# Mixture-of-experts stages: chosen experts only, on rows scattered by place, instead of every expert on every row

## The chip, the cores and the metric

The kernel runs on one core of one Trainium2 chip. The metric is the time of one execution on the device, in microseconds (us). Engines are named as in the profile: PE is TensorE's matmul and PEld its weight load, DVE is VectorE, ACT is ScalarE, POOL is GpSimd, SP is SyncE (here it only starts DMAs).

## The reference

Two transformer layers over 2048 tokens of width 128, all float32. Each layer is an attention and a feed-forward part; layer 0 has a 16-head attention and a routed feed-forward, layer 1 an 8-head attention, a second 16-head attention and a routed feed-forward. The change touches the two routed feed-forwards:

```python
# layer 0: 8 experts, each token takes 2; expert width 384; and one shared expert of width 128
top_v, top_i = jax.lax.top_k(probs, 2)
gates = jax.nn.softmax(top_v, axis=-1)
for e in range(8):
    out = out + comb[:, e, None] * swiglu(normed, gate_up_w[e], down_w[e])   # comb: gate or 0
out = out + swiglu(normed, shared_gate_up_w, shared_down_w)
# layer 1: 4 experts, each token takes 1; expert width 512
expert_idx = jnp.argmax(logits, axis=-1)
for e in range(4):
    gate_raw, value = jnp.split(h @ expert_wv[e], 2, axis=-1)
    y = silu(gate_raw) * value @ expert_proj[e]
    out = out + jnp.where((expert_idx == e)[..., None], y, 0.0)
```

`swiglu(h, wg, wd)` is `(silu(gate) * up) @ wd.T` with `gate, up` the halves of `h @ wg.T`.

## The kernel before

The 2048 tokens are 16 tiles (`NT`) of 128 rows, or 4 blocks (`NB`) of 512 (`BLK`). The program is a chain of stages; in each, every engine runs its own list, tied by semaphores, and a barrier stands between two stages. No scheduler orders anything around the change: each engine does what its list says, in that order. Around a routed feed-forward the stages are `project_norm_route` (output projection, layer norm, transposed and scaled copy `hT` of the normed rows, router logits, and `routing` on DVE, which leaves in `comb` one weight per token and expert, zero for experts not chosen), then `experts`, then a norm (`norm_l2_norm` in layer 0, `final_norm` in layer 1).

`experts` runs twice: tag `e0` with E = 8 experts of NF = 3 chunks of 128 (and the shared expert as a ninth), tag `e1` with E = 4 and NF = 4. It computes every expert on every token. A unit is one expert on one block of 512 tokens. In `up` (L886 to L893) PE multiplies, for each of the NF chunks, the gate and the up weights with 512 columns of `hT` (L891, L892). ACT takes the silu of the gate half (L932), DVE multiplies it with the up half (L950). In `dn` (L895 to L901) PE multiplies 128-column pieces of that product with the down weights (L900), 4·NF matmuls of 128 columns, and DVE's `gather` (L955 to L962) adds the result, times `comb`, to the running sum (L960). PE's list has `up` of a unit ahead of `dn` of the unit before it. Loops over pairs of experts are hardware loops (`Fori`). The weights lie in two slots; SP loads the pair for the next turn (L848 and L849, two DMAs per expert) when the last unit of a slot is done, three quarters of a turn before it is wanted. The first two experts' weights are loaded during the stage that prepares the attention.

Of the kernel before, what the change touches and what calls it, by code (L numbers as in the profile page):

```python
# [16 lines left out]
BF16 = mybir.dt.bfloat16  # L17
ALU = mybir.AluOpType
# [3 lines left out]
P = 128  # L22
# [4 lines left out]
TPB = BLK // P  # L27
HEADS, HD = 16, 8
# [65 lines left out]
def small_head_operands(core, tag, src_T, w, bias, cs, arrived, KS, QS, V, place, kbias, tokens, opening, later):  # L94
# [7 lines left out]
    with ExitStack() as st:  # L102
# [23 lines left out]
        with nc.Block() as block:  # L126
# [9 lines left out]
            @block.gpsimd  # L136
            def _(pool):
                if opening:
                    opening.gpsimd(pool)
                pool.memset(V[:, :, :, HD:], 1.0).then_inc(ones_set, 1)  # L140
                for s in range(NS):
# [499 lines left out]
def routing(dve, act_pair, chain, lg, prob, cand, pick, comb, rank, small, n_exp, top2):  # L641
# [19 lines left out]
    if not top2:  # L661
        first_of(lg, m, comb)
        return
# [20 lines left out]
    step(dve.tensor_tensor(pick[:, 0], pick[:, 0], wide(g1), ALU.mult))  # L684
    step(dve.tensor_tensor(pick[:, 1], pick[:, 1], wide(g2), ALU.mult))
    step(dve.tensor_tensor(comb, pick[:, 0], pick[:, 1], ALU.add))
# [19 lines left out]
def project_norm_route(core, tag, OT, X, XA, hT, comb, w, w_in, E, post_norm, top2):  # L706
# [9 lines left out]
    with ExitStack() as st:  # L716
        sem = lambda n: core.sem(st, f"{tag}_{n}")
        sb = lambda n, s, dt=F32: core.sb(st, f"{tag}_{n}", s, dt)
        N = sb("N", [P, NT, P])
# [4 lines left out]
        pick = sb("pick", [P, 2, NT, E])  # L724
        small = sb("small", [P, 5, NT])
# [7 lines left out]
        with nc.Block() as block:  # L733
# [54 lines left out]
            def _(dve):  # L788
# [39 lines left out]
                routing(dve, (e_in, e_out), chain, lg[:, :, :], prob, cand, pick, comb[:, :, 0:E], w["rank"], small, 0, top2)  # L828
                if top2:
                    chain.link(dve.memset(comb[:, :, E:E + 1], 1.0))  # L830
                chain.settle()


class ExpertTiles:
# [3 lines left out]
    def __init__(self, core, st, tag, gate_up, down, NF, shared):  # L838
        self.gate_up, self.down, self.shared, F = gate_up, down, shared, NF * P
        sb = lambda n, s: core.sb(st, f"{tag}_{n}", s)  # L840
        self.wgu, self.wd = sb("wgu", [P, 2, 2 * F]), sb("wd", [P, 2, NF, P])
        self.sgu, self.sd = (sb("sgu", [P, 2 * P]), sb("sd", [P, P])) if shared else (None, None)
        self.w_in = [core.sem(st, f"{tag}_w_in{s}") for s in range(2)]
        self.s_in = core.sem(st, f"{tag}_s_in")

    def load(self, sp, slot, e):
        one = slice(e, e + 1) if isinstance(e, int) else bass.ds(e, 1)
        sp.dma_start(self.wgu[:, slot, :], self.gate_up[one].rearrange("o d f -> (o d) f")).then_inc(self.w_in[slot], 16)  # L848
        sp.dma_start(self.wd[:, slot, :, :], self.down[one].rearrange("o (c p) n -> p (o c) n", p=P)).then_inc(self.w_in[slot], 16)  # L849

    def load_first(self, sp):
        self.load(sp, 0, 0)
        self.load(sp, 1, 1)
        if self.shared:
            sp.dma_start(self.sgu[:, :], self.shared[0]).then_inc(self.s_in, 16)
            sp.dma_start(self.sd[:, :], self.shared[1]).then_inc(self.s_in, 16)


def experts(core, tag, hT, comb, acc, tiles, E, NF):
# [4 lines left out]
    shared, wgu, wd, sgu, sd, w_in, s_in = (tiles.shared, tiles.wgu, tiles.wd, tiles.sgu, tiles.sd, tiles.w_in, tiles.s_in)  # L864
    with ExitStack() as st:
        sem = lambda n: core.sem(st, f"{tag}_{n}")
        sb = lambda n, s, dt=F32: core.sb(st, f"{tag}_{n}", s, dt)
        gate = sb("gate", [P, 2, BLK])
        prod = sb("prod", [P, 2, NF, BLK])

        gu_ready, gu_free, silu_done, prod_ready = (sem(n) for n in ("gu_ready", "gu_free", "silu_done", "prod_ready"))
        y_ready, y_free = sem("y_ready"), sem("y_free")
        UNITS = 2 * NB
        PAIRS = E // 2

        with nc.Block() as block:
            @block.sync
            def _(sp):
                with sp.Fori(0, PAIRS - 1) as it:
                    for slot in range(2):  # L880
                        sp.wait_ge(y_ready, it * UNITS + NB * (slot + 1))
                        tiles.load(sp, slot, it * 2 + 2 + slot)

            @block.tensor
            def _(pe):
                def up(wts, nf, n, u, b):  # L886
                    for c in range(nf):
                        pe.wait_ge(gu_free, n + c + 1)
                        bank = 2 * ((u * nf + c) % 2)
                        cols = hT[:, b * BLK:(b + 1) * BLK]  # L890
                        pe.matmul(ps[:, bank, :], wts[:, c * P:(c + 1) * P], cols, start=True, stop=True)  # L891
                        pe.matmul(ps[:, bank + 1, :], wts[:, (nf + c) * P:(nf + c + 1) * P], cols,  # L892
                                  start=True, stop=True).then_inc(gu_ready, 1)  # L893

                def dn(wts, nf, n, u, m):  # L895
                    pe.wait_ge(prod_ready, n + nf)
                    pe.wait_ge(y_free, m + 1)
                    for i in range(TPB):
                        for c in range(nf):
                            mm = pe.matmul(ps[:, 4 + u % 2, i * P:(i + 1) * P], prod[:, u % 2, c, i * P:(i + 1) * P],  # L900
                                           wts(c), start=(c == 0), stop=(c == nf - 1))  # L901
                    mm.then_inc(y_ready, 1)

                with pe.Fori(0, PAIRS) as it:
                    n0, m0 = it * (UNITS * NF), it * UNITS
                    for u in range(UNITS):
                        slot = u // NB
                        if u % NB == 0:
                            pe.wait_ge(w_in[slot], it * 32 + 32)
                        up(wgu[:, slot, :], NF, n0 + u * NF, u, u % NB)  # L910
                        if u >= 1:
                            v = u - 1
                            dn(lambda c: wd[:, v // NB, c, :], NF, n0 + v * NF, v, m0 + v)
                    v = UNITS - 1
                    dn(lambda c: wd[:, v // NB, c, :], NF, n0 + v * NF, v, m0 + v)
                if shared:
                    n0, m0 = PAIRS * UNITS * NF, PAIRS * UNITS
                    pe.wait_ge(s_in, 32)
                    for u in range(NB):
                        up(sgu[:, :], 1, n0 + u, u, u)  # L920
                        if u >= 1:
                            dn(lambda c: sd[:, :], 1, n0 + u - 1, u - 1, m0 + u - 1)
                    dn(lambda c: sd[:, :], 1, n0 + NB - 1, NB - 1, m0 + NB - 1)

            @block.scalar
            def _(act):
                def silu(nf, n, u):
                    for c in range(nf):
                        k = (u * nf + c) % 2
                        act.wait_ge(gu_ready, n + c + 1)  # L930
# [863 lines left out]
```

## Time and profile before

| | us |
|---|---|
| three runs, median | 2432.5 |
| three runs, lowest and highest | 2427.86 and 2433.84 |
| the profiled execution | 2438.78 |
| its span, first to last instruction | 2436.9 |
| first expert stage (layer 0, tag e0) | 265.8, from 793.5 to 1059.3 |
| second expert stage (layer 1, tag e1) | 171.9, from 2249.5 to 2421.4 |
| routing on DVE ahead of the first expert stage | from 784.7 to 792.9 |

The profile gives the instructions of one execution with their start and duration, the time an engine sat idle before an instruction and what ended that idle time. A float32 matmul stands in it as two records. The granted clock (PEclk) is the share of TensorE's full 2.4 GHz that was granted; 0.5 is the 1.2 GHz level.

### The profile page before, as it was taken

The page shows a single profiled execution, that of the slowest core. Times are in us where ns is not written, and L with a number is a line of the kernel's source. Part 1 is how long each engine was busy: PE and PEld are TensorE (multiplying, and loading weights), DVE is VectorE, ACT ScalarE, POOL GpSimd, SP SyncE. Part 2 cuts the span into 40 slices and gives each one's busy share as a digit, 9 for nine tenths or more (in the row PEclk, how much of TensorE's full clock was granted, in tenths as well). Part 3 has the DMA queues.
Part 4 walks back from the last instruction along what each step waited for, and adds up shares of the span by engine and source line. Part 5 has one row for each costly group of instructions (what it writes and reads, how often), then busy time and mean ns, then how long its engine had stood idle before and what let it go on. Part 6 is the DMA issues. An engine that isn't in the chain of part 4 may idle for free. (4 is left out here: it accounts for less than half of the span.)

```text
span 2436.9 us, 41652 instructions
## 1 busy us (share of the span) xinstructions
PE 2136.9 (88%) x16528; PEld 1019.0 (42%) x16528; DVE 1684.9 (69%) x2408; ACT 1398.9 (57%) x2564; POOL 208.1 (9%) x366
## 2 busy tenths in 40 slices
PE   7589999999995999968897999996759999996997
PEld 2122222222223566644565776775212323343564
DVE  4799999999944344444765677775479888862334
ACT  3179989899894222234544566563417888773221
POOL 2000000000001000012331111111100000000000
PEclk7589999999997999989998999998659999996998
DMA  3000000000000000000000000001000000000000
GB/s 109 1 3 4 6 4 6 4 6 6 4 6 3 10 20 19 10 35 1 1 1 1 1 1 1 1 1 42 26 1 4 4 6 6 9 10 10 14 13 17
DMA packets 21424, 26.01 MB, mean 11 GB/s; under 512 B 4736, under 2 KB 14976, under 8 KB 21120
## 3 DMA queue, kind: packets, MB, share of 16 engines
q1 hardware_dynamic: 19152, 21.42, 3.1%
q8 instruction: 120, 1.97, 0.3%
q10 hardware_dynamic: 2096, 2.17, 0.3%
q14 instruction: 56, 0.46, 0.1%
HBM read 17.94 MB, written 1.05 MB: 8 GB/s over the span
## 5 line engine op out<-in xcount | busy, mean ns | idle before, releaser
L591 ACT ACTIVATE a0a_probs<-psum 128x512 f32<-128x512 f32 x1024 | 554.0, 596 | 109.2 <-PE psum L531 102.2
L615 DVE TENSOR_REDUCE a0a_mx<-psum 128x2 f32<-128x1024 f32 x512 | 583.2, 1213 | 9.2 <-PE psum L511 8.9
L511 PE MATMUL psum<-a_KS,a_QS 48*128 48x512 bf16 (+3 forms) x1664 | 332.9, 393 | 78.6 <-DVE a0a_mx L615 42.7
L591 ACT ACTIVATE a1a_probs<-psum 128x512 f32<-128x512 f32 (+3 forms) x640 | 304.6, 533 | 118.5 <-PE psum L531 77.7
L615 DVE TENSOR_REDUCE a1a_mx<-psum 128x2 f32<-128x1024 f32 (+2 forms) x320 | 323.8, 1060 | 53.1 <-PE psum L511 30.0
L531 PE MATMUL psum<-a_QS,a_KS 51*128 51x512 bf16 (+3 forms) x1664 | 337.4, 382 | 10.9 <-ACT a1a_probs L591 4.1
L554 PE MATMUL psum<-a0a_probs,a_V 128*16 128x256 f32 x4096 | 327.1, 391 | 7.8 <-ACT a0a_OD L580 5.5
L932 ACT ACTIVATE e_gate<-psum 128x512 f32<-128x512 f32 x164 | 97.9, 597 | 320.7 <-PE psum L892 320.7
L1284 PE MATMUL psum<-b_VW,b_ST 128*128 128x129 f32 x2176 | 256.2, 280 | 16.2 <-DVE X L1395 16.2
L1284 PEld LDWEIGHTS psum<-b_VW,b_ST 128*128 128x128 f32 x2176 | 253.1, 197 | 17.3 <-DVE X L1395 17.3
L1264 PE MATMUL psum<-b_GT,AT 128*128 128x512 f32 (+3 forms) x640 | 244.8, 536 | 16.9 <-ACT b_ST L1323 16.9
L531 PEld LDWEIGHTS psum<-a_QS,a_KS 51*128 51x128 bf16 x1664 | 87.2, 93 | 368.6 <-ACT a0a_probs L591 197.0
L950 DVE TENSOR_TENSOR e_prod<-e_gate,psum 128x512 f32<-128x512 f32 x164 | 112.8, 688 | 181.5 <-ACT e_gate L932 181.5
L1371 DVE TENSOR_TENSOR b_M<-b_M,b_ST 128x512 f32<-128x512 f32 (+3 forms) x288 | 176.0, 611 | 51.6 <-ACT b_ST L1323 19.2
L1264 PEld LDWEIGHTS psum<-b_GT,AT 128*128 128x128 f32 x640 | 122.4, 193 | 154.3 <-issue 115.5
L554 PE MATMUL psum<-a1a_probs,a_V 128*16 128x256 f32 (+1 forms) x2304 | 179.3, 382 | 4.2 <-ACT a1a_OD L580 4.1
L1330 ACT ACTIVATE b_ST<-b_ST 128x2048 f32<-128x2048 f32 x48 | 91.8, 1912 | 153.9 <-DVE b_ST L1379 153.9
L1323 ACT ACTIVATE b_ST<-psum 128x512 f32<-128x512 f32 (+1 forms) x320 | 156.2, 536 | 36.3 <-PE psum L1264 35.1
L900 PEld LDWEIGHTS psum<-e_wd,e_prod 128*128 128x128 f32 x1280 | 149.6, 192 | 20.0 <-issue 20.0
L900 PE MATMUL psum<-e_wd,e_prod 128*128 128x128 f32 x1280 | 149.7, 275 | 0.0
L554 PEld LDWEIGHTS psum<-a0a_probs,a_V 128*16 128x16 f32 x4096 | 68.6, 95 | 193.3 <-issue 99.2
L511 PEld LDWEIGHTS psum<-a_KS,a_QS 48*128 48x128 bf16 x1664 | 83.4, 95 | 149.9 <-DVE a0a_mx L615 76.0
(202 smaller groups left out, 1929.7 us busy)
## 6 DMA issues: line engine op xcount, KB each, us to landing
e_wgu<-in_l_gate_up SPq DMA_DIRECT2D x8, 384.0 KB, 3.0
a_cs<-in_rope ACTq DMA_DIRECT2D x4, 512.0 KB, 9.9
a_cs<-in_rope SPq DMA_DIRECT2D x1, 2048.0 KB, 7.5
e_wgu<-in_l_gate_up SPq DMA_DIRECT2D x4, 512.0 KB, 3.5
e_wd<-in_l_down SPq DMA_DIRECT2D x8, 192.0 KB, 3.0
AT<-in_xT SPq DMA_DIRECT2D x4, 256.0 KB, 6.1
a_QS<-a0a_mrow SPq DMA_DIRECT2D x64, 3.0 KB
a0a_num<-a0a_OD SPq DMA_DIRECT2D x64, 16.0 KB
```

What stands on the lines that cost most here:

```text
L511: mm = pe.matmul(ps[:, 2 * slot + half, 0:width], QS[rows, 2 * p + i, q_cols(qb, qt * P, P)], KS[rows, 2 * p + i, c * BLK:c * BLK + width] ...
L531: mm = pe.matmul(ps[:, S_BANK + e % S_SLOTS, c:BLK], KS[rows, 2 * p + i, kt * P:(kt + 1) * P], QS[rows, 2 * p + i, q_cols(qb, c, BLK - c)] ...
L554: mm = pe.matmul(ps[32 * j:32 * j + 2 * HD, AV_BANK, a:b], V[:, kt, HPP * p + j, :], probs[:, e % P_SLOTS, a:b], start=(kt == 0 and half = ...
L591: act.activation(probs[:, e % P_SLOTS, c:BLK], ps[:, S_BANK + e % S_SLOTS, c:BLK], ACT.Exp, scale=scale).then_inc(exp_done, 1)
L615: dve.tensor_reduce(mx[:, pk % 2, qt, 2 * i:2 * i + 2, c], banks, AX.X, ALU.max).then_inc(max_done, 1)
L900: mm = pe.matmul(ps[:, 4 + u % 2, i * P:(i + 1) * P], prod[:, u % 2, c, i * P:(i + 1) * P], wts(c), start=(c == 0), stop=(c == nf - 1))
L932: act.activation(gate[:, k, :], ps[:, 2 * k, :], ACT.Silu).then_inc(silu_done, 1)
L950: dve.tensor_tensor(prod[:, u % 2, c, :], gate[:, k, :], ps[:, 2 * k + 1, :], ALU.mult).then_inc(prod_ready, 1)
L1264: pe.matmul(ps[:, n % S_BANKS, c:BLK], xnT[:, kt * P:(kt + 1) * P], GT[:, a % 3, c:BLK], start=True, stop=True).then_inc(s_ready, 1)
L1284: mm = pe.matmul(ps[:, O_BANK + i // 2, cols], ST[:, plan.at[a][kt // TPB], kt % TPB, i * P:(i + 1) * P], VW[:, kt, h, :], start=(kt == 0 ...
L1323: act.activation(tile(a, kt), ps[:, n % S_BANKS, c:BLK], ACT.Copy).then_inc(copied, 1)
L1371: dve.tensor_tensor(M[:, a % 2, c:], M[:, a % 2, c:], tile(a, kt), ALU.max).then_inc(max_done, 1)
```

## The change

`ExpertTiles` and `experts` go; `sparse_experts`, with `SharedExpert`, `Route`, `Dispatch` and the constant `dispatch_table`, takes their place. The tokens are cut in two halves (`PARTS`). Within a half, each token is given a row number for each expert it chose (K = 2 in layer 0, 1 in layer 1), such that the rows of one expert stand together and each expert begins at a multiple of 128. That takes at most JT = 8·K + E − 1 tiles of 128 rows: 23 in layer 0 and 11 in layer 1, of which some are empty; all are computed, 46 and 22 in all.

- DVE and PE work out the row numbers (`posi`) and which expert each tile belongs to (`own`): four matmuls and some 14 small DVE operations.
- POOL scatters the normed rows N of each token tile, once per choice, to `xg` in device memory with an indirect DMA (32 in layer 0, 16 in layer 1), and at the end gathers the results from `yg` back, by as many indirect DMAs.
- SP reads the tile's expert number from SBUF into a register, waits until the slot is free (three slots, freed by `y_ready` of the tile three before), and fetches all of that expert's weights with one DMA (now merged in one array, 576 KB in layer 0, 768 KB in layer 1), once for each tile. SP also loads the scattered rows and stores the results in groups of four tiles.
- PE transposes the tile's 128 rows (`turn`), ACT scales them, then `up`, silu, product and `down` run on 128 columns; DVE copies the result to `yout` (`keep`). The choice's weight is applied after the gather (`collect`), in layer 0 by one DVE operation per token tile and choice, in layer 1 by a plain add.
- The shared expert runs ahead of the tiles. `xg` is filled with zeros at the start of the kernel. The last three operations of `routing` and a memset go.

```diff
+                def load_weights(j):
+                    e = sp.value_load(own[0:1, j // JT, j % JT:j % JT + 1], min_val=0, max_val=E - 1)
+                    if j >= SLOTS:
+                        sp.wait_ge(y_ready, S + j - SLOTS + 1)
+                    sp.dma_start(W[:, j % SLOTS, :], weights[bass.ds(e, 1)].rearrange("o p n -> (o p) n")).then_inc(w_in[j % SLOTS], 16)
+                def load_rows(b):
+                    sp.wait_ge(sent[b], 16 * K * PART_TILES)
+                    for c, (lo, hi) in enumerate(CHUNKS):
+                        rows = xg[b][lo * P:hi * P, :].rearrange("(t p) c -> p t c", p=P)
+                        sp.dma_start(xin[:, b, lo:hi, :], rows).then_inc(x_in[b][c], 16)
+                def store(b, g):
+                    lo, hi = GROUPS[g]
+                    sp.wait_ge(y_free, S + JT * b + hi)
+                    rows = yg[b][lo * P:hi * P, :].rearrange("(t p) c -> p t c", p=P)
+                    sp.dma_start(rows, yout[:, b, lo:hi, :]).then_inc(stored[b], 16)
...
+                for b in range(PARTS):
+                    for t in tiles_of(b):
+                        for k in range(K):
+                            pool.indirect_dma_start(xg[b], bass.IndirectOffsetOnAxis(posi[:, k, t:t + 1], 0),
+                                                    route.N[:, t, :], None).then_inc(sent[b], 16)
+                for b in range(PARTS):
+                    pool.wait_ge(stored[b], 16 * len(GROUPS))
+                    for t in tiles_of(b):
+                        for k in range(K):
+                            pool.indirect_dma_start(G[:, k, t, :], None, yg[b],
+                                                    bass.IndirectOffsetOnAxis(posi[:, k, t:t + 1], 0)).then_inc(back[t // TPB], 16)
...
+                def turn(j):
+                    b, i = divmod(j, JT)
+                    for c, (lo, hi) in enumerate(CHUNKS):
+                        if i == lo:
+                            pe.wait_ge(x_in[b][c], 16)
+                    if j >= 2:
+                        pe.wait_ge(x_ready, j - 1)
+                    pe.transpose(ps[:, 6 + j % 2, 0:P], xin[:, b, i, :], core.ident[:, :]).then_inc(turned, 1)
+                def up(j):
+                    n, s = S + j, j % SLOTS
+                    wait_banks(n)
+                    pe.wait_ge(w_in[s], 16 * (j // SLOTS + 1))
+                    pe.wait_ge(x_ready, j + 1)
+                    for half in range(2):
+                        for c in range(NF):
+                            mm = pe.matmul(ps[:, 2 * half + n % 2, c * P:(c + 1) * P],
+                                           W[:, s, half * F + c * P:half * F + (c + 1) * P], xT[:, j % 2, :], start=True, stop=True)
+                    mm.then_inc(gu_ready, 1)
+                def down(j):
+                    n, s = S + j, j % SLOTS
+                    wait_down(n)
+                    for c in range(NF):
+                        mm = pe.matmul(ps[:, 4 + n % 2, 0:P], prod[:, n % 2, c * P:(c + 1) * P],
+                                       W[:, s, 2 * F + c * P:2 * F + (c + 1) * P], start=(c == 0), stop=(c == NF - 1))
+                    mm.then_inc(y_ready, 1)
...
+                turn(0)
+                for j in range(ALL):
+                    if j + 1 < ALL:
+                        turn(j + 1)
+                    up(j)
+                    if j:
+                        down(j - 1)
+                down(ALL - 1)
...
+                        for t in range(g * TPB, (g + 1) * TPB):
+                            ins = dve.scalar_tensor_tensor(out=acc[:, t, :], in0=G[:, k, t, :], scalar=route.small[:, 3 + k, t:t + 1],
+                                                           in1=acc[:, t, :], op0=ALU.mult, op1=ALU.add)
```

The list of SP in the first expert stage, before: the two DMAs of an expert's weights (`e_wgu` gate and up, `e_wd` down) behind one wait for PE.

```order
L848 ISA [waits e0_y_ready]
L848 DMA e_wgu<-in_l_gate_up 128x768
L849 ISA
L849 DMA e_wd<-in_l_down 128x3x128
```

The same list now, at the fifth to seventh tile: `e0_own` is the expert number, `e0_W` the slot, `e0_yout` a group of results.

```order
L943 TENSOR_LOAD e0_own
L943 ISA x2
L946 ISA [waits e0_y_ready]
L946 DMA e0_W<-in_l0_experts 128x1152
L958 DMA yg0<-e0_yout 128x4x128 [waits e0_y_free]
L943 TENSOR_LOAD e0_own
L943 ISA x2
L946 ISA [waits e0_y_ready]
L946 DMA e0_W<-in_l0_experts 128x1152
```

Where SP issued 6 such pairs in the stage (and 2 in advance), it now issues 46 loads, each behind a wait for the `down` three tiles back; the register read stands ahead of the wait.

PE's list in the first expert stage, before (`e_wgu`, `e_wd` weights, `h0T` the transposed rows): the last chunk of one unit's `up`, then the 12 matmuls of `dn`.

```order
L891 MATMUL psum<-h0T,e_wgu 128x512 [waits e0_gu_free]
L892 MATMUL psum<-h0T,e_wgu 128x512
L897 ISA [waits e0_prod_ready]
L900 MATMUL psum<-e_wd,e_prod 128x128 [waits e0_y_free]
L900 MATMUL psum<-e_wd,e_prod 128x128 x11
```

The same list now, one tile and the beginning of the next: `e_xin` are the gathered rows, `e_xT` their transpose.

```order
L1031 MATMUL psum<-ident,e_xin 128x128 [waits e0_x_ready]
L1040 MATMUL psum<-e_xT,e_W 128x128 [waits e0_x_ready,e0_w_in1,e0_prod_ready]
L1040 MATMUL psum<-e_xT,e_W 128x128 x5
L1048 MATMUL psum<-e_W,e_prod 128x128 [waits e0_y_free,e0_prod_ready]
L1048 MATMUL psum<-e_W,e_prod 128x128 x2
L1031 MATMUL psum<-ident,e_xin 128x128 [waits e0_x_ready]
```

Every tile now waits for its own weights (`e0_w_in`), once for 10 matmuls of 128 columns; before, one such wait stood ahead of 4 units of 18 matmuls each.

POOL had nothing in the stage. Its list there now (`d_N` normed rows, `e_posi` row numbers, `e_G` the gathered results):

```order
L981 DMA xg<-d_N,e_posi 2944x128 [waits blank,e0_pos_ready]
L981 DMA xg<-d_N,e_posi 2944x128 x31
L987 DMA e_G<-yg,e_posi 128x128 [waits e0_stored0]
L987 DMA e_G<-yg,e_posi 128x128 x15
L987 DMA e_G<-yg,e_posi 128x128 [waits e0_stored1]
L987 DMA e_G<-yg,e_posi 128x128 x15
```

The first 16 scatters stand ahead of the first tile, and the last 16 gathers behind the last one.

## Rows read from the trace of the kernel before

**Rows 1.** The page: busy time, share of the span and instruction count of each engine.
```profile
PE 2136.9 (88%) x16528; PEld 1019.0 (42%) x16528; DVE 1684.9 (69%) x2408; ACT 1398.9 (57%) x2564; POOL 208.1 (9%) x366
```

**Rows 2.** Busy time by stretch (start:end length, engines, PEclk, DMA share, GB/s): both expert stages.
```profile
793.50:1059.30 265.80, 263.79 (x1200) 162.90 (x1200) 109.29 (x244) 64.84 (x104) 0.00 (x0) 0.99 0.04 14
2249.50:2421.40 171.90, 170.15 (x768) 104.03 (x768) 62.06 (x128) 40.74 (x66) 0.02 (x1) 0.98 0.03 9
```

**Rows 3.** Grouped instructions, first expert stage: count | busy, mean ns | idle before <-releaser.
```profile
L891 PE MATMUL psum<-h0T,e_wgu 128*128 128x512 f32 x192 | 99.8, 601 | 9.1 <-DVEq L942 9.1
...
L900 PE MATMUL psum<-e_wd,e_prod 128*128 128x128 f32 x768 | 90.3, 275 | 0.0
...
L932 ACT ACTIVATE e_gate<-psum 128x512 f32<-128x512 f32 x100 | 59.7, 597 | 197.7 <-PE psum L892 197.7
```

**Rows 4.** In order of time (start, duration): a unit boundary in the first expert stage.
```profile
854.81 3.74 PE L900 MATMUL psum<-e_wd,e_prod 128*128 128x128 f32 x32
...
858.75 0.34 SPq L848 DMA_DIRECT2D e_wgu<-in_l_gate_up  x1
...
859.27 0.38 SPq L849 DMA_DIRECT2D e_wd<-in_l_down  x1
...
868.72 2.84 PE L900 MATMUL psum<-e_wd,e_prod 128*128 128x128 f32 x24
```

**Rows 5.** DMA issues: KB each, median us from issue to landing.
```profile
e_wgu<-in_l_gate_up SPq DMA_DIRECT2D x8, 384.0 KB, 3.0
...
e_wgu<-in_l_gate_up SPq DMA_DIRECT2D x4, 512.0 KB, 3.5
...
e_wd<-in_l_down SPq DMA_DIRECT2D x4, 256.0 KB, 3.9
...
out_tokens<-XA SPq DMA_DIRECT2D x4, 256.0 KB, 2.2
big_raw<-in_l_big_wq SPq DMA_DIRECT2D x1, 512.0 KB, 3.5
...
big_raw<-in_l_big_wo SPq DMA_DIRECT2D x1, 512.0 KB, 6.1
a_wk<-in_l_wk SPq DMA_DIRECT2D x2, 64.0 KB, 1.8
```

**Rows 6.** SP's queue in order of time, first and last of four 512 KB loads.
```profile
1059.54 0.34 SPq L1005 DMA_DIRECT2D big_raw<-in_l_big_wq  x1
...
1060.88 0.43 SPq L1005 DMA_DIRECT2D big_raw<-in_l_big_wo  x1
```

**Rows 7.** POOL's groups over the whole span, columns as in rows 3.
```profile
L1215 POOL PARTITION_ALL_REDUCE b_row<-b_M x32 | 57.0, 1783 | 33.1 <-DVE b_M L1371 27.4 <-issue 5.7
...
L740 POOL TENSOR_TENSOR r_scales<-r_both,r_half 128x4 f32<-128x4 f32 x4 | 4.1, 1030 | 9.7 <-DVE r_both L802 9.7
```

**Rows 8.** DVE in order of time, end of the first routing.
```profile
792.14 0.29 DVE L685 TENSOR_TENSOR r_pick<-r_pick,r_small 128x128 f32<-128x128 f32 x1
792.47 0.29 DVE L686 TENSOR_TENSOR comb<-r_pick 128x128 f32<-128x128 f32 x1
```

**Rows 9.** Four PE transposes of 128x128, in order of time.
```profile
768.85 0.66 PE L756 MATMUL psum<-ident,r_N 128*128 128x128 f32 x4 [3.49 <-DVE r_N L816]
```

**Rows 10.** Groups over the whole span, 128x384 and 128x128 forms on ACT and DVE.
```profile
L1371 DVE TENSOR_TENSOR b_M<-b_M,b_ST 128x384 f32<-128x384 f32 x32 | 19.1, 596 | 8.5 <-POOL b_ST L1207 7.0
...
L591 ACT ACTIVATE a1a_probs<-psum 128x128 f32<-128x128 f32 x64 | 14.2, 275 | 9.4 <-PE psum L487 9.4
```

**Rows 11.** Busy time by stretch, columns as in rows 2: stretches that bear on TensorE's clock.
```profile
302.00:305.40 3.40, 1.71 (x22) 0.42 (x14) 3.40 (x2) 2.81 (x6) 0.00 (x0) 1.00 0.00 0
306.00:312.00 6.00, 4.50 (x30) 0.72 (x34) 4.93 (x5) 1.47 (x3) 0.00 (x0) 0.50 0.00 0
1139.00:1142.50 3.50, 1.97 (x5) 0.66 (x5) 1.88 (x5) 2.03 (x5) 0.00 (x0) 1.00 0.00 0
795.00:797.00 2.00, 2.00 (x4) 0.82 (x3) 0.00 (x0) 0.00 (x0) 0.00 (x0) 0.50 0.00 0
```

More of the change, by code:

```diff
@@ L827, in _ @@
                 chain.settle()
[L828 to L843, printed above, removed]
-        self.s_in = core.sem(st, f"{tag}_s_in")
[L846 to L856, printed above, removed]
@@ new lines, in _ @@
+                sp.wait_ge(own_ready, 1)
+                for j in range(SLOTS):
+                    load_weights(j)
+                load_rows(0)
+                stores = [(JT * b + GROUPS[g][1], b, g) for b in range(PARTS) for g in range(len(GROUPS))]
+                for j in range(SLOTS, ALL):
+                    if j % JT == JT - GROUP and j // JT + 1 < PARTS:
+                        load_rows(j // JT + 1)
+                    load_weights(j)
+                    while stores and stores[0][0] + SLOTS <= j:
+                        store(*stores.pop(0)[1:])
@@ new lines, in _ @@
+                for _, b, g in stores:
+                    store(b, g)
+            @block.gpsimd
+            def _(pool):
+                pool.wait_ge(pos_ready, 1)
+                pool.wait_ge(*blank)
+                for b in range(PARTS):
[9 more added lines that the diff above has]
+                                                    bass.IndirectOffsetOnAxis(posi[:, k, t:t + 1], 0)).then_inc(back[t // TPB], 16)
@@ L933, in _, with silu @@
[L933 to L938 removed]
+                def silu(n, width):
+                    act.wait_ge(gu_ready, n + 1)
+                    if n >= 2:
+                        act.wait_ge(prod_ready, n - 1)
+                    act.activation(gate[:, n % 2, 0:width], ps[:, n % 2, 0:width], ACT.Silu).then_inc(silu_done, 1)
@@ L955, in gather @@
-                def gather(m, u, b, e):
-                    dve.wait_ge(y_ready, m + 1)
-                    one = slice(e, e + 1) if isinstance(e, int) else bass.ds(e, 1)
-                    for i in range(TPB):
-                        t = b * TPB + i
-                        ins = dve.scalar_tensor_tensor(out=acc[:, t, :], in0=ps[:, 4 + u % 2, i * P:(i + 1) * P],
-                                                       scalar=comb[:, t, one], in1=acc[:, t, :],
-                                                       op0=ALU.mult, op1=ALU.add)
-                    ins.then_inc(y_free, 1)
@@ L964, in _ @@
[L964 to L976 removed]
+                chain = Chain(dve, sem("chain"))
@@ new lines, in _ @@
+                for u in range(S):
+                    product(u, BLK)
+                    if u:
+                        add_shared(u - 1)
+                if S:
+                    add_shared(S - 1)
+                at = {JT + JT // 2 + 1: 0, JT + 3 * JT // 4 + 1: 1} if PARTS == 2 else {}
+                for j in range(ALL):
+                    product(S + j, F)
+                    if j:
+                        keep(j - 1)
+                    if j in at:
+                        collect(at[j])
@@ L1646, in two_layers @@
         forward = list(range(NB))
+        rows = (PART_TILES * 2 + 7) * P
+        xg, yg = ([nc.dram_tensor(f"{n}{b}", (rows, P), F32, kind="Internal").ap() for b in range(PARTS)] for n in ("xg", "yg"))
         with ExitStack() as layer:
```

326 lines of the change are left out of this document (220 added, 106 removed).

## Prediction

> **What bounds the kernel now.** I looked first at the engines' busy shares, then at the stages the change touches. PE is busy 88% of the span [rows 1], but only the two expert stages matter here. There the view by stretch shows PE busy 263.8 of 265.8 us and 170.2 of 171.9 us, while DVE and ACT are busy under half of the time and the DMA engines 4% [rows 2]. The reader is to see that both stages are bound by PE at the full clock (0.99 and 0.98), and that weight traffic is nothing: each expert's weights serve 2048 rows. The groups of the first stage say what fills PE: matmuls of 512 columns (the one line shown, and its twin for the up half), and 768 records (384 matmuls) of 128 columns [rows 3]. So fewer rows through PE do shorten these stages, until something else is late. Of 8 (4) experts, 2 (1) are needed per token; with padding the change computes 46 tiles of 128 rows where 128 stood, and 22 where 64 stood.
>
> **Price of a tile on PE.** In order of time, 24 records (12 matmuls of 128 columns) take 2.84 us and 32 take 3.74 us, 0.234 us a matmul with its weight load hidden [rows 4]. Four transposes take 0.66 us with the tail of the last, which I read as 0.12 us each [rows 9]. A tile of layer 0 is one transpose, 6 `up` and 3 `down`: 0.12 + 9·0.234 = 2.23 us. In layer 1 it is 0.12 + 12·0.234 = 2.93 us. ACT's silu and scaling (two operations between 0.28 and 0.60 us) and DVE's product and copy (0.60 us for 128x384, some 0.3 us for 128x128) come to under 1.1 us a tile [rows 3, 10] and hide behind that. Were PE the bound, the loops would take 46·2.23 = 103 and 22·2.93 = 64 us.
>
> **Price of a tile by its weights.** Every tile now fetches its own weights, and load j may start only when `down` of tile j−3 is done. Four 512 KB loads were issued between 1059.54 and 1060.88 [rows 6]; the first landed 3.5 us and the last 6.1 us after its issue [rows 5], that is at 1063.0 and 1067.0: three further loads in 3.95 us, 1.3 us for 512 KB. So a load costs 2.2 us fixed and 1.3 us per 512 KB: 3.67 us for 576 KB and 4.15 us for 768 KB. (As two DMAs 0.52 us apart the 768 KB took 0.52 + 3.9 = 4.4 us [rows 4, 5]; that is my upper end.) To it come 0.16 us from the last matmul's issue to its end (275 ns of one record against 117 ns spacing [rows 3, 4]), 0.2 us from that end to SP's issue (858.55 to 858.75 [rows 4]), and an estimated 0.1 us to wake PE: 4.13 and 4.61 us. In PE's list there lie between `down` of tile j−3 and `up` of tile j one whole period and one transpose. The period is so 4.13 − 0.12 = **4.0 us** in layer 0 and **4.5 us** in layer 1, against 2.23 and 2.93 us of PE work. The weights, not PE, end each wait. SP's register read is new and in no row; it stands ahead of the wait and has some 3 us to hide in.
>
> The Trainium skill, "DMA: Bandwidth & Descriptors", section "Anatomy of one DMA — SWDGE (gpsimd) path", fits a DMA to 2.0 us plus its bytes at 436 GB/s; as an estimate that is 3.35 and 3.8 us a load, and by it the two loops would be some 23 us shorter. The row with 512 KB (3.5 us where the fit says 3.2) is longer than that.
>
> **Loops.** 46·4.0 = 184 and 22·4.5 = 99 us. Stores of 256 KB (0.65 us of the DMA engines each at the rate above) and the loads of further rows share the DMA engines with the weights, 12 and 6 stores: I add 6 and 3 us. Loops: 190 and 102 us.
>
> **What stands ahead of the first tile.** (a) Row numbers: 9 small DVE steps of about 0.32 us spacing (0.33 us from 792.14 to 792.47 for the like [rows 8]), some wider, and two trips to PE: 5.0 us, in layer 1 4.5. (b) 16 scatters on POOL in layer 0, 8 in layer 1; the shared expert (10 us on PE) runs beside them and is hidden, and so are the first three weight loads. The trace shows no indirect DMA. Ends: SP's issue of a DMA, 0.33 us [rows 4], and the longest software operation of POOL, 1.78 us; a tiny POOL power takes 1.03 us [rows 7]. It cannot be below nothing, since POOL does nothing here now. I take **1.3 us**, between the two POOL rows because POOL builds each of the 128 row transfers itself: 20.8 and 10.4 us. (c) The last scatter lands (2.2 us, as a store to device memory), the first three tiles of rows are loaded (between 1.8 us for 64 KB and 3.0 for 384 KB [rows 5], 2.4), transposed and scaled (0.8): 5.4 us.
>
> **What stands behind the last tile.** `down` and copy 1.1 us (1.3), store 2.2, gathers of the second half on POOL 20.8 (10.4), landing 2.2, the last sums 2.8 (0.7): 29.1 and 16.8 us. The gathers of the first half run beside the second half's tiles and cost nothing while the loop is this slow.
>
> **The sum.** Layer 0: 5.0 + 20.8 + 5.4 + 190 + 29.1 = 250.3 against 265.8, −15.5. Layer 1: 4.5 + 10.4 + 5.4 + 102 + 16.8 = 139.1 against 171.9, −32.8. `routing` loses three steps, −1.0 [rows 8]. Zero-filling `xg` (3 MB) happens in the opening, where nothing of the next 700 us waits for it: 0. Together −49.3 us: the profiled execution's 2438.8 becomes 2389.5. It stands 6.3 us above the median of the three runs, so I forecast **2384**.
>
> **What each unknown is worth.** 48 indirect DMAs lie on the path: 1 us more on each is 48 us. The loops have 68 tiles: 0.1 us more on each is 7 us. POOL's ends give −47 and +23; the loads' ends (3.5 us as for 512 KB, 0.25 us more as for two DMAs) −12 and +17.
>
> **Rivals.**
> 1. *POOL is cheap.* 0.6 us an indirect DMA: 48·0.7 = 34 us less, **2350**. For it: SP issues in 0.33 us. Against: POOL's own rows. The Trainium skill, "SBUF — State Buffer", section "A bandwidth-pool intuition that's wrong (but worth ruling out)", states 620 ns for a DMA of this kind alone, and 3100 ns beside a DVE copy that holds the port which POOL needs; by the first the time would be 2351, by the second 2470. No row here shows either.
> 2. *POOL is dear: slower than before.* If a scatter or gather of 128 rows costs over 2.3 us, the 48 on the path eat the whole gain; at 2.6 us the time is **2446**. For it: an all-reduce takes 1.78 us and a power on 4 columns 1.03 us [rows 7], so 128 separately addressed rows may well cost more; and DVE works beside it, on the shared expert's products. Against: nothing but those same rows' size.
> 3. *The clock falls.* With the tail of its matmuls counted as the profile counts it, PE would be about 2.5 of 4.0 us busy in layer 0's loop. A stretch with about 55% busy (1139 to 1142.5) keeps the full clock; one with 50% busy (302 to 305.4) is followed by one at half (306 to 312), which ends while PE is full; and the first 2 us after the idle time ahead of the first expert stage run at half (795 to 797) [rows 11]. [...] At 1.2 GHz a tile's PE work is at most doubled, 4.5 and 5.9 us, so at most 0.5·46 + 1.4·22 = 54 us more; but then PE is full, which is what brings the clock back. I take half: **2410**.
> 4. *The loads hide.* Had weight loads no effect, the loops would run at PE's pace, 81 + 35 = 116 us less: **2268**. Against: no row of such a size lands under 3.5 us, and only three slots are there.
> 5. *SP is late.* If the register read and its checks took over 3.3 us, SP would set the period; at 4.5 us in layer 0 that is 23 us more, and with 1 us for each store and row load, which stand in the same list, some 13 more: **2420**.
>
> **How the numbers follow.** Chances: forecast 0.47 (its own range 2355 to 2412), cheap POOL 0.19, dear POOL 0.13, clock 0.11, loads hidden 0.03, SP late 0.07. Range **2325 to 2440**: it takes in POOL's lower end together with 12 us from the loads, and reaches beyond the clock and SP cases; loads hidden and most of dear POOL are left out. A measurement of this kernel tells 0.3% (7.3 us) from no change. Faster by more: 0.82. Within: 0.05. Slower by more: 0.13.
>
> **What would show it.** Right: the DMA queue moving some 45 MB of weights; in both loops PE busy 55 to 65%, its idle time ended by the weights' DMA, and tiles 4.0 and 4.5 us apart; `y_ready` to SP's issue 0.2 us and issue to landing 3.6 and 4.2 us; two stretches of some 20 us in the first stage and two of 10 us in the second in which only POOL works. Wrong: idle time of PE ended by ACT or DVE (then the chain within a tile is the bound), POOL's spacing outside 1.0 to 1.8 us, or SP's issue long after `y_ready`.

## The result and the profile after

The changed kernel took **2336.6 us** (median of 4 runs, 2334.42 to 2344.91) against 2432.4 (4 runs, 2427.86 to 2433.84): ratio 0.9616, 95% interval 0.9589 to 0.9642. The forecast was 2384; the gain is 96 us where 48 were forecast. The profiled execution took 2337.2 us, its span is 2335.4.

From the page of the changed kernel, the engines' shares and the DMA issues (KB each, median us to landing):

```profile
PE 1899.2 (81%) x16048; PEld 934.0 (40%) x16048; DVE 1591.9 (68%) x2242; ACT 1364.8 (58%) x2536; POOL 300.5 (13%) x463
...
e_W<-in_l_experts SPq DMA_DIRECT2D x46, 576.0 KB, 4.0
e_W<-in_l_experts SPq DMA_DIRECT2D x22, 768.0 KB, 4.4
```

PE lost 238 us of busy time [rows 1], and 44 MB of weights are loaded in the two stages. The two expert stages cut into what stands ahead of the first tile, the loop, and what stands behind it (windows of the changed kernel; span of each, busy time of the engines, granted clock, DMA share, GB/s):

```profile
789.84:820.93 31.09, 15.77 (x58) 9.48 (x59) 9.99 (x23) 4.23 (x7) 19.54 (x20) 0.72 0.35 114
820.93:980.24 159.31, 114.18 (x870) 105.89 (x871) 39.20 (x107) 42.76 (x91) 26.73 (x29) 0.95 0.67 206
980.24:1008.49 28.25, 0.44 (x4) 0.25 (x3) 4.88 (x17) 0.00 (x0) 15.10 (x16) 0.56 0.17 44
2193.46:2214.44 20.98, 2.92 (x10) 2.04 (x11) 3.02 (x15) 0.60 (x2) 12.50 (x13) 0.50 0.51 173
2214.44:2304.24 89.80, 70.45 (x548) 67.34 (x548) 20.71 (x45) 23.66 (x44) 10.67 (x12) 0.93 0.62 201
2304.24:2319.73 15.49, 0.00 (x0) 0.00 (x0) 1.72 (x3) 0.00 (x0) 7.56 (x9) 0.63 0.17 47
```

Beside the forecast's terms:

| us | forecast | measured |
|---|---|---|
| layer 0, ahead of the first tile | 31.2 | 31.1 |
| layer 0, 46 tiles | 190 | 159.3 |
| layer 0, behind the last tile | 29.1 | 28.3 |
| layer 1, ahead | 20.3 | 21.0 |
| layer 1, 22 tiles | 102 | 89.8 |
| layer 1, behind | 16.8 | 15.5 |
| both stages | 389.4 | 344.9 |

The four outer terms are right within 2 us. The two loops hold 43 of the 44.5 us by which the stages beat the forecast. Outside the stages the span is 8.7 us shorter: `routing` 2.3, the first stage of the kernel 2.7, and 4.8 in layer 1's projections and small-head attention, of which 1.1 go back elsewhere. The last two are no work of the change. In the thirteen changed and experimental kernels profiled here, whose code there is the same, that stretch of layer 1 takes either some 510 us (seven of them, 509.2 to 510.8) or some 515 (six, 514.9 to 515.5; before 514.95), and the first norm stage starts anywhere from 754.2 to 760.9 (before 760.0). Each kernel has one profile, so whether this falls by chance or goes with the kernel is not shown.

Why a tile takes less than forecast can be read off three tiles. PE's list in layer 0's loop, changed kernel (start, duration, line; in brackets the idle time before it and what ended it). Each tile is a transpose (L1031), `up` (L1040), and the `down` (L1048) of the tile before:

```profile
899.52 1.58 PE L1040 MATMUL psum<-e_xT,e_W 128*128 128x128 f32 x12 [1.79 <-issue]
900.94 0.83 PE L1048 MATMUL psum<-e_W,e_prod 128*128 128x128 f32 x6
901.61 0.27 PE L1031 MATMUL psum<-ident,e_xin 128*128 128x128 f32 x1
902.50 1.58 PE L1040 MATMUL psum<-e_xT,e_W 128*128 128x128 f32 x12 [0.63 <-DVE e_prod L1135]
903.92 0.83 PE L1048 MATMUL psum<-e_W,e_prod 128*128 128x128 f32 x6
904.59 0.27 PE L1031 MATMUL psum<-ident,e_xin 128*128 128x128 f32 x1
905.99 1.58 PE L1040 MATMUL psum<-e_xT,e_W 128*128 128x128 f32 x12 [1.12 <-DVE e_prod L1135]
```

and SP's list beside it:

```profile
901.95 0.34 SPq L946 DMA_DIRECT2D e_W<-in_l_experts  x1
...
904.93 0.34 SPq L946 DMA_DIRECT2D e_W<-in_l_experts  x1
```

The `down` that ends at 901.77 frees a slot; 0.18 us later SP issues the load; the `up` that needs it starts at 905.99, 4.04 us after the issue. But that `down` stands right behind the `up` of 899.52, and from there to 905.99 are **two** tiles: 6.47 = 2.25 (`up` and `down`) + 0.18 + 4.04. The tile between them, at 902.50, waited 0.63 us for a load of its own, which had been under way since 897.80 and landed at 902.41. The profile puts that wait down to `e_prod`, which was done before 900.94; the weights had come last. It is so nearly everywhere: of the 29 tiles from the fourth on in layer 0 for which the trace has the landing, 27 begin `up` 0.09 us after it. Two loads are in flight beside each other, and half of the 6.47 us is a tile's share. In general, with s slots, s − 1 distances = `up` + `down` (2.25 in layer 0, 2.92 in layer 1) + 0.18 to the issue + landing + 0.09, or 2.5 us + landing in layer 0.

### The profile page after: what moved, and what is told of

Read it like the earlier page. It is cut to its first block and busy times, and to the rows that moved or that the text cites. A ratio compares the mean times of both kernels' runs of the same rounds, so it can differ in the third digit from the quotient of the medians.

```text
span 2335.4 us, 40174 instructions
## 1 busy us (share of the span) xinstructions
PE 1899.2 (81%) x16048; PEld 934.0 (40%) x16048; DVE 1591.9 (68%) x2242; ACT 1364.8 (58%) x2536; POOL 300.5 (13%) x463
## 5 line engine op out<-in xcount | busy, mean ns | idle before, releaser
L620 DVE TENSOR_REDUCE a1a_mx<-psum 128x2 f32<-128x1024 f32 (+2 forms) x320 | 323.7, 1060 | 51.9 <-PE psum L516 29.1
L1135 DVE TENSOR_TENSOR e_prod<-e_gate,psum 128x384 f32<-128x384 f32 (+1 forms) x72 | 43.4, 602 | 220.5 <-ACT e_gate L1074 220.5
L1040 PE MATMUL psum<-e_xT,e_W 128*128 128x128 f32 x904 | 126.3, 296 | 64.3 <-issue 39.8
L1040 PEld LDWEIGHTS psum<-e_xT,e_W 128*128 128x128 f32 x904 | 115.8, 206 | 75.9 <-issue 43.5
L1582 DVE TENSOR_TENSOR b_ST<-b_ST,b_row 128x2048 f32<-128x2048 f32 x48 | 107.8, 2288 | 40.8 <-POOL b_row L1418 40.8
```

Source lines behind the costliest of these rows:

```text
L620: dve.tensor_reduce(mx[:, pk % 2, qt, 2 * i:2 * i + 2, c], banks, AX.X, ALU.max).then_inc(max_done, 1)
L1040: mm = pe.matmul(ps[:, 2 * half + n % 2, c * P:(c + 1) * P], W[:, s, half * F + c * P:half * F + (c + 1) * P], xT[:, j % 2, :], start=True ...
L1582: dve.tensor_tensor(group, group, row[:, a % 2, :].unsqueeze(1).broadcast_to([P, TPB, BLK]), ALU.subtract).then_inc(wide_sub, 1)
```

## The experiments

Three theories of the distance between tiles. **One load at a time**, the prediction's: distance = landing + 0.1. **Two in turn**, the rule just read: 2·distance = 2.5 + landing. **Transfer rate**: 576 KB cannot come more often than every 3.4 us. All edits are to the changed kernel, and its 2336.6 us are what they are set beside.

### Four slots

```diff
-    SLOTS = 3
+    SLOTS = 4
```

> One change: the expert stages' weights have 4 slots in place of 3, so that the load of tile j is issued after the down of tile j-4. Three theories of what sets the tiles' distance (3.47 us in layer 0, 4.06 us in layer 1 in the changed kernel). One load at a time, as the prediction had it: distance = landing + 0.1 with three slots, half of that with four, so TensorE's own work sets it, 2.55 us and 3.2 us. Two in turn: the up of tile j waits for a load that was issued after the up and down that began with the up of tile j-2, so two distances = 2.5 + landing (4.0 to 4.6 us), with four slots three distances, 2.2 to 2.4 us, again under TensorE's work: 2.55 to 2.8 and 3.2 us. Both give 46 x 0.8 + 22 x 0.9 = 57 us less, 2280 us (2270 to 2295). Transfer rate (576 KB cannot land faster than every 3.4 us): no gain, 2337 us.

Measured: 2281.2 us (ratio to before 0.9379, 0.9364 to 0.9394). The loops take 122.1 and 67.9 us. Loads land later, 5.1 us in the median, and yet tiles come 2.26 us apart (median; mean 2.64). The transfer rate is no bound at 3.4 us: it falls. The other two forecast the same here, so this run does not choose between them.

### No loads in the loop

```diff
                 for j in range(SLOTS, ALL):
                     if j % JT == JT - GROUP and j // JT + 1 < PARTS:
                         load_rows(j // JT + 1)
-                    load_weights(j)
...
-                    pe.wait_ge(w_in[s], 16 * (j // SLOTS + 1))
+                    pe.wait_ge(w_in[s], 16)
```

> Leaves out the loads of weights from the fourth tile of each expert stage on, with their register reads: tiles use what the first three loads left in the slots. If the loads set the tiles' distance, what is left is TensorE's work of a tile with the turn of the next, 2.55 to 2.8 us in layer 0 and 3.2 us in layer 1: 2280 us (2270 to 2295). If the chain turn, scale, up, Silu, product, down sets it, the distance stays at 3.4 to 3.5 us and the time at 2337 us.

Measured: 2256.0 us (0.9273, 0.9259 to 0.9287). PE's list without loads:

```profile
849.92 1.50 PE L1039 MATMUL psum<-e_xT,e_W 128*128 128x128 f32 x12
851.26 0.83 PE L1047 MATMUL psum<-e_W,e_prod 128*128 128x128 f32 x6
851.93 0.27 PE L1030 MATMUL psum<-ident,e_xin 128*128 128x128 f32 x1
852.04 1.50 PE L1039 MATMUL psum<-e_xT,e_W 128*128 128x128 f32 x12
```

and the loop's window:

```profile
817.57:917.17 99.60, 99.09 (x872) 98.70 (x872) 38.75 (x107) 42.83 (x91) 26.78 (x29) 0.99 0.25 74
```

PE is full, 2.12 us a tile (2.79 in layer 1), under the 2.23 of the prediction and well under the 2.55 that I had written for this run, which is why the time is 14 us under the range expected. Nothing but the loads, with SP's register reads, stands between the changed kernel's 159.3 us and 99.6: the chain of ACT and DVE within a tile is hidden.

### Half of each load

```diff
-                    sp.dma_start(W[:, j % SLOTS, :], weights[bass.ds(e, 1)]...
+                    n = 3 * F if j < SLOTS else 3 * F // 2
+                    sp.dma_start(W[:, j % SLOTS, 0:n], weights[bass.ds(e, 1), :, 0:n]...
```

> From the fourth tile of each expert stage on only the first half of the weights' columns is loaded (288 and 384 KB); the rest of a slot keeps what the first loads brought. Landing should fall from 4.0 to about 3.25 us and from 4.4 to about 3.4 us. One load at a time (distance = landing + 0.1): 3.35 and 3.5 us, 2336.6 - 46 x 0.12 - 22 x 0.56 = 2319 us. Two in turn (distance = (2.5 + landing)/2, layer 1 (3.2 + landing)/2): 2.9 and 3.3 us, 2336.6 - 26 - 17 = 2294 us. Transfer rate: half the distance, so TensorE's own, 2280 us.

Measured: 2301.8 us (0.9449, 0.9431 to 0.9468). Window of layer 0's loop:

```profile
821.44:955.01 133.57, 108.42 (x872) 101.28 (x872) 39.02 (x107) 42.77 (x91) 26.77 (x29) 0.98 0.54 150
```

Landing fell to 3.1 us, tiles come 2.77 us apart in the median (mean 2.89); two in turn says (2.5 + 3.1)/2 = 2.8. The loop lost 25.7 us where 26 were expected by that theory and 5.5 by the other, and layer 1's lost 13.9 of 17. The total is 8 us over the 2294: 3 are those of layer 1, and the profiled execution has the 515 us form of the stretch named above; the rest is not accounted for. One load at a time falls: the distance, 2.77 us, is under the landing of 3.1, as it was under it in the changed kernel (3.35 and 4.0). A landing 0.86 us shorter took 0.57 us off a tile (by the medians), where the rule gives 0.43: it fits the level better than the slope.

### Two slots

```diff
-    SLOTS = 3
+    SLOTS = 2
```

> Two slots in place of three: the load of tile j is issued after the down of tile j-2, and the up of tile j follows it at once, so distance = TensorE's 2.3 (3.0) + 0.2 + landing: with 3.4 to 4.0 us of landing 5.9 to 6.5 us in layer 0, with 4.0 to 4.4 us 7.2 to 7.6 us in layer 1: 2336.6 + 46 x 2.7 + 22 x 3.3 = 2533 us (2515 to 2555). If the transfer rate sets the distance (3.4 us per 576 KB), one load at a time still lands in under 3.4 us and the loss is smaller than 100 us.

Measured: 2661.4 us (1.0937, 1.0917 to 1.0957, from two runs), over 100 us above every theory. PE's and SP's lists, and the loop's window:

```profile
905.75 2.90 PE L1040 MATMUL psum<-e_xT,e_W 128*128 128x128 f32 x12 [3.78 <-issue]
908.45 1.49 PE L1048 MATMUL psum<-e_W,e_prod 128*128 128x128 f32 x6
909.73 0.42 PE L1031 MATMUL psum<-ident,e_xin 128*128 128x128 f32 x1
913.80 2.90 PE L1040 MATMUL psum<-e_xT,e_W 128*128 128x128 f32 x12 [3.65 <-issue]
```

```profile
910.11 0.34 SPq L946 DMA_DIRECT2D e_W<-in_l_experts  x1
```

```profile
824.20:1188.22 364.02, 190.97 (x869) 177.38 (x870) 42.02 (x107) 42.82 (x91) 26.70 (x29) 0.64 0.30 92
```

`up` and `down` take 4.19 us where they took 2.25: PE runs at 1.2 GHz, and it is busy only 191 of 364 us even so. 4.19 + 0.17 + 3.69 = 8.05 us is the distance from 905.75 to 913.80; at the full clock it would be 6.1, within what was expected. The landing (3.7 us) is what was expected too. So the rule holds, and the miss is the clock, granted at 0.64 over this loop: the prediction's third rival, which did not come with three slots (0.95 granted, PE 72% busy), came in the run with the longer waits. No run keeps the longer waits and the lower clock apart; the 6.1 us are worked out, not measured.

### Every load twice

```diff
-        W = sb("W", [P, SLOTS, 3 * F])
+        W = sb("W", [P, SLOTS, 6 * F])
...
+                    sp.dma_start(W[:, j % SLOTS, 3 * F:6 * F], weights[bass.ds(e, 1)]...
```

> Every load of weights is done twice, the second time into a second half of a slot that nobody reads; a tile waits for both. Three slots. Landing of the later of the two perhaps 5.5 us (layer 0) and 6.4 us (layer 1). Two in turn: distances (2.5 + 5.5)/2 = 4.0 and (3.2 + 6.4)/2 = 4.8 us: 2336.6 + 46 x 0.5 + 22 x 0.75 = 2377 us; the check is the sum by the landing that the profile then shows. One load at a time: distance = landing + 0.1, 5.6 and 6.5 us: 2336.6 + 98 + 54 = 2490 us. Transfer rate (twice the distance): 2336.6 + 160 + 89 = 2585 us.

Measured: 2453.1 us (1.0084, 1.0055 to 1.0113, from two runs), under the 2490 and 2585 of the other two and 76 above the 2377. Tiles come 4.85 us apart in the median. From its first issue to the `up` a pair of loads took 6.2 us in the median, so 6.1 to landing, not 5.5; with that, two in turn gives 4.3 at the full clock and 5.3 at half, and the clock was 0.80 in this loop. The mean distance is 5.27, since two tiles at its start came 13.6 and 9.3 us after their neighbours and a later one 12.7, which no theory of the loads covers; more of that below. The run speaks against one load at a time (6.2) but is too disturbed to measure the slope.

### One part in place of two halves

```diff
-PARTS = 2
+PARTS = 1
```

> All the rows as one part in place of two halves: 39 and 19 tiles in place of 46 and 22, but all 32 and 16 scatters stand ahead of the first tile and all 32 and 16 gathers behind the last. At 1.26 us for each indirect transfer of 128 rows: 16 and 8 more on either side, 48 x 1.26 = +60 us; 7 x 3.45 and 3 x 4.06 us of tiles less, -36 us: 2336.6 + 24 = 2361 us (2350 to 2370). If GpSimd's transfers weren't what the stage's head and tail wait for: 2336.6 - 36 = 2300 us.

Measured: 2357.8 us (0.9688, 0.967 to 0.9706), 3 us from the expectation. Windows of layer 0, ahead, loop, behind:

```profile
792.23:843.44 51.21, 15.47 (x58) 9.48 (x59) 9.66 (x23) 4.24 (x7) 31.15 (x32) 0.63 0.26 89
843.44:975.59 132.15, 96.77 (x739) 89.36 (x739) 29.42 (x77) 36.18 (x77) 0.00 (x0) 0.95 0.64 194
975.59:1023.57 47.98, 0.00 (x0) 0.00 (x0) 9.46 (x33) 0.00 (x0) 30.32 (x32) 0.54 0.18 48
```

20.1 us more ahead and 19.7 behind for 16 indirect transfers each: 1.25 us a piece, all on the path. In layer 1 it is 9.1 and 10.1 for 8 each. The halves hide 48 transfers, worth 59 us, for ten padded tiles, 40 us.

### Plain transfers in place of indirect ones

```diff
-    pool.indirect_dma_start(xg[b], bass.IndirectOffsetOnAxis(posi[:, k, t:t + 1], 0), route.N[:, t, :], None)
+    pool.dma_start(xg[b][at:at + P, :], route.N[:, t, :])
...
-    pool.indirect_dma_start(G[:, k, t, :], None, yg[b], bass.IndirectOffsetOnAxis(posi[:, k, t:t + 1], 0))
+    pool.dma_start(G[:, k, t, :], yg[b][at:at + P, :])
```

> Scatters and gathers by GpSimd are plain transfers of the same 128 rows to and from fixed places, in place of indirect ones; the rows thus go to tiles by place and not by expert. 48 of the 96 stand on the path (16 + 16 + 8 + 8), 1.26 us each. If the price is that of reading 128 indices, a plain one should take GpSimd 0.6 us or less: at least 48 x 0.65 = 31 us less, 2305 us or under. If it is that of any transfer that GpSimd issues: 2337 us.

Measured: 2311.5 us (0.9497, 0.9479 to 0.9515). POOL's list of the changed kernel, then of this one:

```profile
808.70 0.96 POOL L981 DMA_INDIRECT xg<-d_N,e_posi  x1 [0.30 <-issue]
809.96 0.96 POOL L981 DMA_INDIRECT xg<-d_N,e_posi  x1 [0.30 <-issue]
```

```profile
797.91 17.16 POOL L982 DMA_DIRECT2D xg<-d_N  x32 [20.28 <-DVE e_posi L1121]
```

An indirect transfer of 128 rows holds POOL for 1.26 us, a plain one to or from 128 rows that stand together for 17.16/32 = 0.54. So 0.72 of the 1.26 us go with the indices and the scattered places, which this run changes together; the time is 6 us over the bound expected for that case and 26 under the other. Of 48·0.72 = 35 us, 24 came out at the stages' ends (7.9, 11.7, 1.1 and 3.7). Least came ahead of layer 1's first tile, where POOL was no longer last: it had issued the eighth scatter by 2187.1, but that landed at 2193.26, beside the first three loads of weights (2184.85 to 2196.0), and SP loads the rows behind it. Over both stages a plain scatter landed after 4.7 us where the indirect one took 2.6 (medians).

### More slots, and a stall

> Six slots for the weights. With four the loop's distances were 2.12 us where TensorE went at its own pace and 2.64 in the mean (layer 1 2.79 and 3.02). Loads that are issued five tiles ahead should be covered: 46 x 0.45 + 22 x 0.15 = 24 us less than with four slots, 2257 us, which is what the kernel without loads took (2256). If many loads in flight only slow each other and the rows' stores, the time stays at 2281 us.

Measured with `SLOTS = 6`: 2299.0 us (0.9455, 0.9433 to 0.9477), slower than with four. Most tiles do come 2.12 us apart, but three of them 10.9, 9.2 and 14.8 us after their neighbours. ACT's list there, and what its waits were put down to over the stage:

```profile
833.74 0.49 ACT L1074 ACTIVATE e_gate<-psum 128x384 f32<-128x384 f32 x1 [9.25 <-remote]
837.26 0.46 ACT L1080 ACTIVATE e_xT<-psum,columns 128x128 f32<-128x128 f32 x1 [3.03 <-PE psum L1031]
844.31 0.49 ACT L1074 ACTIVATE e_gate<-psum 128x384 f32<-128x384 f32 x1 [6.59 <-remote]
...
ACT e_gate L1074 <- remote: 30.5, 4, 12.2
```

and beside it one `down` on PE, POOL's last scatter and SP's next load:

```profile
834.88 1.65 PE L1048 MATMUL psum<-e_W,e_prod 128*128 128x128 f32 x6 [6.44 <-issue]
...
838.62 0.96 POOL L981 DMA_INDIRECT xg<-d_N,e_posi  x1 [0.31 <-issue]
...
844.53 3.09 SPq L946 DMA_DIRECT2D e_W<-in_l_experts  x2
```

The silu at 833.74 needed the `up` that had ended at 826.99; from 828.4 on, when PE has done one more `up`, POOL's list alone goes on. In the second stall SP stands as well: its load at 844.53 waited for the `down` that had ended at 836.53, where 0.18 us is usual. POOL's last scatter was over at 839.58, yet ACT and SP went on only at 844.3 and 844.5, so POOL's being busy is not by itself what holds them. Four further runs asked what does it.

> With six slots, and with every load done twice, the first tiles of layer 0 came 10.9 and 9.2 us apart while GpSimd issued the second half's scatters, and one more 14.8 us after its neighbour while GpSimd issued the first half's gathers; ScalarE began its Silu and its scale late there. Both kernels hold 27 KB of weights in a partition where the changed kernel holds 14, so that all tiles behind W lie 14 KB further on. Here W has six slots but stands behind all the others, and 3 slots of unused room stand where W stood: the other tiles keep the changed kernel's places. If the places decide, no such stall: 2256 us (2250 to 2262). If the number of loads in flight decides, 2299 us.

Six slots, but `W` stands behind all other tiles and unused room of three slots in its old place: 2264.5 us (0.9306, 0.9285 to 0.9326), 2 us over the range of the first theory, without the stall. The loops take 106.2 and 64.1 us.

> Three slots used as in the changed kernel, but W is declared with six, so that all the tiles behind it lie where the kernel with six slots has them. If the places decide, the changed kernel's time and the stalls of some 20 and 15 us that six slots showed: 2360 us (2350 to 2375). If the number of loads in flight decides: 2337 us.

Three slots used, `W` declared with six: 2343.3 us (0.9621, 0.9598 to 0.9644), loops 158.1 and 89.3 us as in the changed kernel, without the stall; its profiled execution has the stretch outside the stages in its long form (515.5 us against 510.2). So neither the tiles' places alone nor the number of loads alone does it.

> Six slots, and the scatters of the second half are left out (its tiles take the zeros, or what an earlier layer left, in their place). If GpSimd's scatters beside the tiles are what holds ScalarE up, the first tiles of layer 0 come 2.1 us apart, 16 us less, and the stall beside the gathers stays: 2299 - 16 = 2283 us. If the stall has nothing to do with them: 2299 us.

Six slots without the second half's scatters: 2261.2 us (0.929, 0.9266 to 0.9313, from two runs). The stall beside the scatters is gone, but so is the one beside the gathers, which was to stay: the time is 22 us under the lower of the two expectations.

> Five slots. Without the stalls of six the loop would be covered nearly always: 2281 - 15 = 2266 us (2260 to 2272), which would be the fastest version. With the stalls of six: 2300 us.

Five slots: **2265.8 us** (0.9303, 0.9285 to 0.932). Window of layer 0's loop and of layer 1's:

```profile
822.01:931.88 109.87, 103.45 (x872) 102.01 (x872) 38.79 (x107) 42.75 (x91) 26.71 (x29) 0.96 0.87 287
2169.21:2232.18 62.97, 62.45 (x543) 62.27 (x544) 20.52 (x45) 23.66 (x44) 8.88 (x10) 0.97 0.75 256
```

The cause of the stall stays open. It showed only in the two kernels in which `W` takes the room of six slots in front and more than three loads' worth of data is under way (six slots, and every load twice), during or within 5 us of POOL's indirect transfers, and it reads as ACT and SP standing still. With places alone, loads alone, or without the second half's scatters it is absent. No run names a mechanism.

The distances together, layer 0 (landing: median; rule: (s − 1)·distance = work + 0.27 + landing):

| kernel | slots | landing | rule | median | mean |
|---|---|---|---|---|---|
| two slots (1.2 GHz) | 2 | 3.7 | 8.2 | 8.1 | 7.98 |
| changed kernel | 3 | 4.0 | 3.25 | 3.35 | 3.47 |
| half of each load | 3 | 3.1 | 2.8 | 2.77 | 2.89 |
| four | 4 | 5.1 | 2.5 | 2.26 | 2.64 |
| five | 5 | 5.6 | 2.12 (PE) | 2.12 | 2.36 |
| none loaded | | | 2.12 (PE) | 2.12 | 2.13 |

With four slots some tiles wait and some run at PE's pace, and the rule lies between median and mean. In layer 1 of the changed kernel it gives (2.92 + 0.27 + 4.4)/2 = 3.8 us, and the mean is 4.06: two loads there landed 5.6 and 5.9 us after their issue, and twice `up` and `down` took 4.5 us together.

## Why the prediction was right in direction and half in size

- **Bounds of before.** Right. PE filled both stages [rows 2], and PE's work per tile is 2.12 us (2.79) where the prediction took 2.23 (2.93). Its 0.234 us a matmul holds the tail of the last one; the difference of the two rows in [rows 4], (3.74 − 2.84)/4 = 0.225, gives 2.15 and 2.82.
- **The loops: the step that failed.** "In PE's list there lie between `down` of tile j−3 and `up` of tile j one whole period and one transpose. The period is so 4.13 − 0.12 = 4.0". The count of PE's work is right, but one idle time was left out: behind `down` of tile j−3 comes the `up` of tile j−1, and it too waits for its load, so that one period, one transpose and a second wait lie there. Counted from the start of the `up` of tile j−2, which stands ahead of that `down`, two periods hold the work of one tile and one landing. With the prediction's own numbers that is (2.11 + 4.13)/2 = 3.12 us and (2.81 + 4.61)/2 = 3.71: 58 us less, a forecast of 2326. Measured were 3.47 and 4.06 in the mean. The lists of PE and SP that stand ahead of the prediction were enough to find this.
- **Landing.** 3.67 and 4.15 us were taken, 4.0 and 4.4 measured, each transfer beside another in flight; that gives back 0.17 us on each of 46 tiles and 0.12 on each of 22, 10 us. 2326 + 10 = 2336, the measured time. That it meets is luck: the loops so corrected are still 5 us short of the measured ones, the rest of the kernel took 9 us less than forecast, and the 6.3 us taken off for the profiled execution of before were 0.6 after (2389.5 − 6.3 is, besides, 2383 and not 2384). Part of what the loops lack lies where the second half's row loads stand ahead of a load of weights in SP's list. SP needed 2.31 us to issue that load where 0.34 is usual, it landed at 891.56, and tiles there came 4.3, 5.7 and 3.8 us apart:

```profile
881.03 0.34 SPq L946 DMA_DIRECT2D e_W<-in_l_experts  x1
881.42 2.68 SPq L952 DMA_DIRECT2D e_xin<-xg  x3
884.85 2.31 SPq L946 DMA_DIRECT2D e_W<-in_l_experts  x1
```

- **POOL.** 1.3 us an indirect transfer was a guess between two rows [rows 7] that have nothing to do with it; 1.26 was measured, so that term is right by luck. All 48 on the path cost what the sum said. The rivals with POOL cheap (0.6) and dear (2.6) are out. The Trainium skill, "SBUF — State Buffer", section "A bandwidth-pool intuition that's wrong (but worth ruling out)", has 620 ns for a DMA that GpSimd issues, alone, and 3100 beside a DVE copy; it does not speak of an indirect one. By the trace an indirect one is 960 ns plus 300 of issue, and it was that too beside DVE's products and copies, which here read PSUM; no run has the 3100. The plain transfer's 540 ns are near the 620.
- **Row numbers, landing, tail.** Right in sum: 31.1 against 31.2 and 28.3 against 29.1 us. In layer 0 the row numbers took 5.8 us and not 5.0, and from the last scatter to the first tile it was 5.0 and not 5.4. SP's register read stood in the waits' shadow, and SP issued 0.18 us after `down` (0.2).
- **The clock.** It fell in neither loop with three slots (0.95, 0.93), PE being 72% and 78% busy in them, not 55 to 65% as the prediction had it at the longer period. With two slots it did (0.64).
- **Loads hidden.** Against its rival of 2268 the prediction said that "only three slots are there". With three it didn't come; with five it did, at 2265.8.
- **Outside the stages** `routing` gave 2.3 us, not 1.0, and 7.5 more came in stages that the change does not touch. The profiled execution of before had stood 6.3 us above its median, so span and median part by as much.

## What to carry to other kernels

In a ring of s buffers that the consumer itself frees, write the list of the consumer with every one of its waits, and count from the last wait that stands ahead of the step that frees the buffer (here that of the `up` of tile j−s+1) to the wait for the load. With a list like this one, (s − 1) distances hold one unit's work and one latency. A third buffer brought the distance from work + latency to half of that, and a fourth and fifth took the latency out altogether (here 71 us more, for 9 KB of each partition in layer 0's stage and 12 KB in layer 1's). A longer wait can be paid twice: with two slots TensorE's part of a tile took 4.19 us in place of 2.25, at a granted clock of 0.64.

## What the runs showed of the hardware

- An indirect transfer of 128 rows of 512 bytes holds POOL for 0.96 us and 0.30 us of issue, a plain one of the same size for 0.54 in all.
- A load of 576 KB landed in 3.3 us at the least and 3.7 in the median with one in flight, 4.0 in the median with two, 5.1 and 5.6 with three and four (slots 2, 3, 4 and 5); the loop with five slots drew 287 GB/s.
- In the loop of 364 us with two slots, PE being busy for 191 of them, the granted clock was 0.64, and PE's part of the tile shown took 4.19 us in place of 2.25.
- ACT, and SP with it, stood still for up to 12 us beside or just behind POOL's indirect transfers in two kernels, by a combination of places and traffic that the runs don't resolve.
